# Writing f by pairs of images and moving the last f products ahead of the taps

## What is computed

```python
def first(x):                      # x = x + first(group_norm(x))
    f = relu(conv1x1(x, conv_w) + conv_b)                   # 256 -> 64 channels
    g = relu(mean_pixels(x) @ conv_w.T + conv_b)            # (16, 64)
    K = g[:, :, None] * wk + bk                             # a 5x5 kernel per image and channel
    W1 = relu(k0 * K + k1 * K.mean(0) + kb)                 # and W2, 3x3, in the same way
    y1 = depthwise(f, W1, 5x5) + adap_bias
    y2 = depthwise(f, W2, 3x3, dilation 2) + atrous_bias
    return conv1x1(concat(y1, y2), fuse_w) + fuse_b         # 128 -> 256 channels

def second(x):                     # x = x + second(group_norm(x))
    ...                            # halo attention, blocks of 8 x 8, windows of 16 x 16
    sim = where(mask, -max, q @ k + rel_pos)                # mask: positions inside the image
    out = softmax(sim) @ v @ Wout.T + Wout_b
```

## Time and profile before

| | |
|---|---|
| runs shown | 208.17, 208.6 and 210.85 us (median 208.6) |
| the profiled execution | 205.92 us, its span from first to last instruction 204.0 us |
| TensorE busy | 162.2 us, 80% of the span |
| VectorE, ScalarE, GpSimd busy | 151.0, 126.4, 89.0 us |
| bytes moved | 54.82 MB, mean 269 GB/s |
| chain that ended last | TensorE 64%, SyncE's queue 26%, copies of f 3% |

### The profile page before, as it was taken

How to read it: one execution, slowest core, us unless ns; L and a number is a source line. 1 busy time by engine, 2 the same in 40 slices (tenths; PEclk the granted TensorE clock), 3 DMA queues, 4 the chain that set the end, 5 groups by cost and what they waited for, 6 DMA issues and landing times.

```text
span 204.0 us, 3894 instructions
## 1 busy us (share of the span) xinstructions
PE 162.2 (80%) x1376; PEld 101.3 (50%) x1376; DVE 151.0 (74%) x342; ACT 126.4 (62%) x241; POOL 89.0 (44%) x139
## 2 busy tenths in 40 slices
PE   0001696966597999999999999999999999999430
PEld 0000322322256375676586676586586587584330
DVE  0198948888492418989989789899789899799930
ACT  2667469989346264775695585695495695444520
POOL 8802305050508304124337557328857417527530
PEclk9999999999999999999999999999999999999955
DMA  6999999999499999999637679996999998972997
GB/s 207 406 410 409 410 408 410 409 395 252 132 192 206 229 212 224 220 223 209 147 77 176 136 258 210 309 289 159 322 291 239 280 339 209 335 276 112 381 358 282
DMA packets 24466, 54.82 MB, mean 269 GB/s; under 512 B 2560, under 2 KB 14592, under 8 KB 22912
## 3 DMA queue, kind: packets, MB, share of 16 engines
q1 hardware_dynamic: 24032, 54.14, 87.5%
q10 hardware_dynamic: 416, 0.44, 0.9%
HBM read 32.78 MB, written 21.79 MB: 268 GB/s over the span
## 4 chain that ended last, share of the span: by engine, by line
PE 64%; SPq 26%; DMA 3%; issue 2%; ACT 1%; DVE 1%; POOL 1%; DVEq 0%; ACTq 0%
PE pt L819 29%; PE pf L831 28%; SPq L203 14%; SPq L215 9%; PE pf L757 3%; DMA fc<-fd 3%; PE px L856 3%; SPq L208 2%; PE px L845 1%; ACT junkt L455 1%; POOL cw L398 1%; SPq L224 0%; SPq L206 0%; DVE xs L182 0%; DVEq L66 0%
## 5 line engine op out<-in xcount | busy, mean ns | idle before, releaser
L458 ACT ACTIVATE junkt<-xs,sm 128x1024 bf16<-128x1024 f32 x31 | 35.6, 1149 | 37.7 <-DVE xs L672 37.7
L831 PE MATMUL pf<-reg,cst 128*128 128x512 f32 x128 | 58.8, 603 | 0.0
L672 DVE SCALAR_TENSOR_TENSOR xs<-pf,cst,xs 128x1024 f32<-128x1024 f32 x31 | 39.5, 1273 | 7.0 <-PE pf L831 7.0
L418 ACT ACTIVATE wa<-xs 128x1024 bf16<-128x1024 f32 x28 | 29.3, 1053 | 10.3 <-DMA xs<-x_dram 10.3
L654 DVE STREAM_TRANSPOSE reg<-pt 128x512 f32<-128x512 f32 x32 | 23.0, 717 | 17.1 <-PE pt L819 14.1
L831 PEld LDWEIGHTS pf<-reg,cst 128*128 128x128 f32 x128 | 23.0, 190 | 24.9 <-issue 24.4
L329 POOL TENSOR_TENSOR pre<-cst,sv 96x512 f32<-96x512 f32 x15 | 15.8, 1056 | 43.7 <-ACT wa L442 19.6
L819 PEld LDWEIGHTS pt<-fc,wa 96*64 96x64 f32 x512 | 27.8, 136 | 7.1 <-issue 5.3
L819 PE MATMUL pt<-fc,wa 96*64 96x128 f32 x512 | 29.8, 274 | 1.4 <-DMA fc<-fd 1.4
L819 PEld LDWEIGHTS pt<-fc,reg 96*64 96x64 f32 x512 | 27.9, 136 | 5.9 <-issue 5.9
L819 PE MATMUL pt<-fc,reg 96*64 96x128 f32 x512 | 29.7, 273 | 0.0
(11 more groups left out here) (102 smaller groups left out, 130.8 us busy)
## 6 DMA issues: line engine op xcount, KB each, us to landing
xs<-x_dram SPq DMA_DIRECT2D x16, 1024.0 KB, 18.6
fc<-fd SPq DMA_DIRECT2D x48, 306.0 KB, 5.3
out_dram<-xs SPq DMA_DIRECT2D x10, 1024.0 KB, 6.1
out_dram<-xs SPq DMA_DIRECT2D x12, 256.0 KB, 4.6
out_dram<-xs SPq DMA_DIRECT2D x6, 512.0 KB, 3.6
fd<-own SPq DMA_DIRECT2D x40, 76.5 KB, 5.6
fd<-reg SPq DMA_DIRECT2D x24, 76.5 KB, 4.6
cst<-columns_dram ACTq DMA_DIRECT2D x1, 304.0 KB, 4.3
```

The costliest lines, as they stand in the source:

```text
L418: act.activation(junkl[m % 2], plane(n, c), func, scale=scale, accum_out=dst).then_inc(s_xs, 1)
L458: act.activation(junk[m % 2], plane(n, c), ACT.Square, bias=nwb[:, c:c + 1], accum_out=accq[:, 1, m:m + 1]).then_inc(s_sq, 1)
L672: dve.scalar_tensor_tensor(out=plane(n, c), in0=pf[c][:, :], scalar=fb[:, c:c + 1], in1=plane(n, c), op0=ALU.add, op1=ALU.add, accum_out=r ...
L831: mm = pe.matmul(pf[c][:, h * HALF:(h + 1) * HALF], fw[:, 128 * c:128 * (c + 1)], y2[n % 2][:, h * HALF:(h + 1) * HALF], start=True, stop= ...
```

## The change

It does six things.

- The attention weights and `sx` get room of their own at the end of `reg`; their loads stay behind x in the queue.
- f is written to DRAM by pairs of images: one transfer of 128 partitions x 8 x 153 numbers in place of eight of 16 x 8 x 153. The channels of the convolution are permuted on the host so that the planes fall into place.
- A copy of f goes to partitions k, k + 4, k + 8, ... (k = 0, 1, 2) in place of 32 neighbours. The taps' operations run over 128 partitions in place of 96; every fourth partition has weights and data of zero. For that GpSimd sets both copy buffers to zero as a whole, ahead of its other memsets.
- TensorE's order changes: the attention product comes right after the first half of f pair 5, and pairs 6 and 7 come ahead of the taps of image 0.
- ScalarE's order follows: the attention matrix ahead of the taps' fourth channel, pairs 5 and 6 ahead of the weights of image 1.
- GpSimd's scaled weights of the last batch wait for the pixel means.

```diff
-KROWS = 96
+KROWS = 128
...
-        reg = sb("reg", [128, 3072 + WALL])
+        reg = sb("reg", [128, 3072 + WALL + 96])
...
-        wv, wot = fc[1][:, 0:512], fc[1][:, 512:1024]
-        sx = fc[1][0:64, 1024:1536].rearrange("p (n g v) -> p n g v", n=N, v=2)
+        wv, wot = reg[:, 3672:4184], reg[:, 4184:4696]
+        sx = reg[0:64, 4696:5208].rearrange("p (n g v) -> p n g v", n=N, v=2)
...
-            sp.wait_ge(s_fcz, 2)
             sp.dma_start(wv.rearrange("p (k c) -> p k c", k=2),
...
-            def write_f(n):
-                sp.wait_ge(s_fev, n // 2 + 1)
-                m = 64 * (n % 2)
-                for c4 in range(4):
-                    sp.dma_start(bass.AP(fd, n * IMG + c4 * SPLIT * SET, [[PLANE, GROUPS], [SET, SPLIT], [1, PLANE]]),
-                                 slots[n // 2][m + c4:m + c4 + 61:4, :].rearrange("p (h f) -> p h f", h=SPLIT)
-                                 ).then_inc(s_fw[n], 16)
+            def write_f(q):
+                sp.wait_ge(s_fev, q + 1)
+                sp.dma_start(bass.AP(fd, 2 * q * IMG, [[PLANE, 2 * CM], [2 * CM * PLANE, SPLIT], [1, PLANE]]),
+                             slots[q].rearrange("p (h f) -> p h f", h=SPLIT)).then_inc(s_fw[q], 16)
...
                 for k in range(3):
-                    sp.dma_start(fc[n % 2][32 * k:32 * k + 32, LEAD - k:LEAD - k + RUN],
-                                 bass.AP(fd, n * IMG, [[SET, 32], [1, RUN]])).then_inc(s_cp[n % 2], 16)
+                    sp.dma_start(fc[n % 2][k:k + 125:4, LEAD - k:LEAD - k + RUN],
+                                 bass.AP(fd, n // 2 * 2 * IMG + n % 2 * CM * PLANE,
+                                         [[2 * CM * PLANE, SPLIT], [SET, 4], [1, RUN]])).then_inc(s_cp[n % 2], 16)
...
             for b in range(2):
-                pool.memset(fc[b][:, RUN:COPY], 0.0).then_inc(s_fcz, 1)
+                pool.memset(fc[b][:, :], 0.0).then_inc(s_fcz, 1)
...
                 pool.wait_ge(s_rstd, k + 1)
+                if k == BATCHES - 1:
+                    pool.wait_ge(s_gm, BATCHES)
...
-            for q in range(2, 6):
+            for q in range(2, 5):
                 store_f(q)
+            act.wait_ge(s_atm, 1)
+            act.activation(at[:, :], pf[0][:, 0:HALF], ACT.Copy, scale=1.0 / KEYS).then_inc(s_at, 1)
...
+            store_f(5)
+            store_f(6)
             taps(1)
-            store_f(6)
             store_f(7)
```

More of the change, by code:

```diff
@@ L146, in build @@
         s_attw = sem("attention_weights_loaded")
-        s_fw = [sem(f"f_written{n}") for n in range(N)]
+        s_fw = [sem(f"f_written{q}") for q in range(N // 2)]
         s_cp = [sem(f"copies_landed{b}") for b in range(2)]
@@ L243, in inner_rows @@
                 store_rows(n, IN0, IN1)
-            for n in range(6):
-                write_f(n)
+            for q in range(2):
+                write_f(q)
+            sp.wait_ge(s_fcz, 2)
             copies(0)
[L248 to L251, removed]
             copies(1)
-            write_f(8)
-            write_f(9)
+            for q in range(2, 7):
+                write_f(q)
             for n in range(N):
@@ L658, in order_image @@
                 if n < 2:
-                    for q in range(2, 6):
-                        dve.wait_ge(s_fw[q], 64)
+                    for q in range(1, 3):
+                        dve.wait_ge(s_fw[q], 16)
                 else:
@@ L777, in _ @@
             f_pair(5, (0,))
[L778 to L787, removed]
-            pe.wait_ge(s_fev, 4)
-            pe.matmul(pf[0][0:KROWS, HALF + 64:HW], sel, flat[:, 64:512], start=True, stop=True).then_inc(s_smm, 1)
-            for c in range(NC2):
-                pe.matmul(pt0[:, 96 + c:97 + c], fw[:, 128 * c:128 * (c + 1)], yb, start=True, stop=True)
-            shifts(3)
-            pe.wait_ge(s_attw, 32)
+            pe.wait_ge(s_attw, 32)
+            pe.wait_ge(s_fev, 4)
             for c in range(NC2):
@@ L798, in _ @@
             mm.then_inc(s_atm, 1)
+            pe.wait_ge(s_gm, BATCHES)
+            for c in range(NC2):
+                mm = pe.matmul(px[:, 64:64 + N], cw[:, c, :], gm[:, c, :], start=(c == 0), stop=(c == NC2 - 1))
+            mm.then_inc(s_gmm, 1)
+            shifts(3)
+            for c in range(NC2):
+                pe.matmul(pt0[:, 96 + c:97 + c], fw[:, 128 * c:128 * (c + 1)], yb, start=True, stop=True)
+            pe.wait_ge(s_sx, 1)
+            flat = reg[0:64, 4696:5208]
+            pe.matmul(px[0:KROWS, 0:64], sel, flat[:, 0:64], start=True, stop=True).then_inc(s_smm, 1)
+            f_pair(5, (1,))
+            pe.wait_ge(s_sx, 2)
+            pe.matmul(pf[0][0:KROWS, HALF + 64:HW], sel, flat[:, 64:512], start=True, stop=True).then_inc(s_smm, 1)
+            f_pair(6)
+            f_pair(7)
             def taps(n, h):
@@ L906 @@
     mask16 = np.zeros((128, GROUPS), np.float32)
-    for ch in range(CM):
-        mask16[ch, ch // 4] = 1.0
-        for p in range(KROWS):
-            if p % 32 // 8 == ch % 4:
-                sel[ch, p] = 1.0
+    for q in range(CM):
+        mask16[q, q % GROUPS] = 1.0
+        for k in range(3):
+            sel[q, 4 * (q // GROUPS) + k:KROWS:16] = 1.0
+    perm = 4 * (np.arange(CM) % GROUPS) + np.arange(CM) // GROUPS
     group_mean = (row[:, None] // GROUP == row[None, :] // GROUP).astype(np.float32) / GROUP
```

27 lines of the change are left out of this document (10 added, 17 removed).

## The result

| | before | changed |
|---|---|---|
| median of the runs | 208.38 us (207.26 to 210.85, 4 runs) | 212.53 us (210.06 to 213.75, 4 runs) |
| ratio, 95% interval | | 1.0158 (1.0106 to 1.0211) |
| profiled execution, its span | 205.92 us, 204.0 us | 211.46 us, 209.5 us |
| start of the taps of image 1 | 73.34 us | 74.98 us |
| start of the taps of image 2 | 80.47 us | 84.34 us |

The changed kernel is 1.6% slower. The forecast was 209.5 us with a range up to 211.3, so the measured median lies above the range; one of the four runs, 210.06, lies inside it.

The account below looks back on a forecast made before the run. The end was taken to hang on when the taps of image 1 start, with TensorE at a fixed pace after. -3.1 (TensorE's order) + 4.0 (memset) = +0.9 us on 208.6 gave 209.5 us, range 204.4 to 211.3.

Parts of the forecast that it names:

- the memset holds VectorE: At the start, GpSimd's longer memsets hold VectorE's first constants from 9.48 to 13.4 us: +4.0 us.
- nothing takes the delay up: From VectorE's constants to TensorE's list: no wait absorbs the late start, so all 4.0 us arrive there.
- +0.9: Sum of the terms for the whole kernel: -3.1 us from TensorE's order and +4.0 from the memset.
- TensorE's order: Ahead of the taps, reordered products fill idle waits; taps of image 1 start at 70.25 against 73.34, 3.1 us earlier.
- f products at 0.215 us a record: TensorE ahead of the taps: each f product costed at 6.87 / 32 records, 1.72 us for a half pair.
- I take zero for all of this, and the cover is the 6.87 us of f products: Copies of images 0 and 1 land before needed, under cover of f pairs 6 and 7: no cost.
- a gap between tap groups: Named sign of a wrong forecast: gaps opening between TensorE's tap groups would mean copies come late.
- The rival that was priced by rate alone: Copies split over 8 of 16 transfer engines exceed 7.28 us an image: +25 us, 234 us; chance 0.06.
- 10.9 us with 5.3: Copies, in the half-engines rival: 10.9 us from issue to need, 5.3 to landing, some 5.6 us of lead.
- SyncE issues less: SyncE issues half a write of f per image in place of four, so its own time falls; counted as zero.

Follow-up runs that it names:

- run 3: Changed kernel with the two whole memsets of the copy buffers on VectorE ahead of its constants, not on GpSimd: 213.02 us, ratio 1.0301.
- run 10: Changed kernel with all edits of run 8, and f pairs 5, 6, 7 written behind the copies of images 2, 3, 4: 202.31 us, ratio 0.9776.
- run 7: Changed kernel with f pairs 6 and 7 back behind the taps of image 0 and the copy-buffer memsets on VectorE: 211.0 us, ratio 1.0136.
- run 2: Changed kernel with f written per image in two transfers per pair, so copies use all 16 engines: 207.9 us, ratio 1.0017.
- run 9: Changed kernel with only the writes of f pairs 5, 6, 7 moved behind the copies of images 2, 3, 4; copies on 8 engines: 215.33 us, ratio 1.0304.
- run 8: Changed kernel with copies on 16 engines, copy-buffer memsets on VectorE, and second half of f pair 5 right behind the means product: 208.79 us, ratio 1.0077.
- run 11: As run 10, but copies and writes of f keep the changed kernel's form, so copies run on 8 engines: 208.19 us, ratio 0.9911.

## Why the prediction was wrong

**Right: the memset holds VectorE.** 4.20 us were forecast as 4.0, and 13.4 us as its end. The sentence that nothing takes the delay up was too strong: 2.9 of it arrive ahead of the taps. That the taps of image 1 come 1.6 us late where +0.9 was forecast is in part luck: 1.1 us less from the memset stand against 1.8 more from the clock below. The Trainium skill ("SBUF — State Buffer", section "Who interferes with whom") says that a tensor_scalar can be held by a GpSimd instruction for its whole length; this trace agrees with 4.20 us beside the memset and 0.17 without it (run 3).

**Right: TensorE's order.** The engine followed the list, with the wait of 0.70 us ahead of the scales. In run 10, without memset and half clock, the taps of image 1 start 4.0 us earlier than before, which is the forecast's 3.1, the 0.70 of the gap that the filler closes, and 0.2 more.

**Left out: the granted clock.** The terms took f products at 0.215 us a record throughout. Behind products of 1 to 64 columns and a gap of 0.70 us the clock went to its lower level: +1.8. No row of before shows such a fall at that place, but its list had full products between the small ones, and the new list does not.

**The step that failed: "I take zero for all of this, and the cover is the 6.87 us of f products".** The step followed the copies of images 0 and 1 alone, and these were in time. The copies of image 2 wait for a buffer that the taps of image 0 free. Before, the f products of pairs 6 and 7 stood between those taps and the taps of image 2, which made 80.47 - 66.47 = 14.0 us, and the copies, issued from 69.29, still had 11.2 of it:

```profile
69.29 2.23 SPq L224 DMA_DIRECT2D fc<-fd  x3
```

Now the products stand ahead of both, and 82.05 - 74.95 = 7.1 are left, while the copies need 84.30 - 75.01 = 9.3 from first issue to landing. The products cannot cover the load of image 0 and that of image 2 at once. It cost 2.3 us of wait and 1.7 of half clock behind it, and those 4.0 us are what turns +1.6 into +5.6. It is the sign of being wrong that the prediction named: a gap between tap groups. The short window alone is not the cause: in run 10 one of 7 us was enough, and in run 7 one of some 14 was not. It takes the window and the late landing together.

**The rival that was priced by rate alone.** Copies on half of the engines had a chance of 0.06, with the condition that they decide where an image's transfers exceed 7.28 us. They do not: from 89.66 on no image waits, and in all the split cost 1.4% (run 2). The split itself came as that rival said; the Trainium skill ("DMA: Bandwidth & Descriptors", section "Why a DMA increments its semaphore by 16 and not by 1") has the rule, the largest number up to 16 that divides both outermost counts, and the trace agrees with 8 small packets a copy. What decided was the time from issue to landing of one set of copies, once, in a window of 7.1 us: 9.3 us, and 8.8 with nothing ahead of it in run 9. The prediction did compare a window with a landing time, 10.9 us with 5.3, but both were those of the kernel before; the change itself shortens the one and lengthens the other.

**SyncE's queue.** The prediction counted that SyncE issues less. It did not count what now stands ahead of the copies of image 2, two pair writes of 612 KB that used to stand behind. In the changed kernel that hides behind the slow copies; in run 8 it is worth 6.5 us.

**Open.** Each of the three edits of run 8 was not taken out of run 10 by itself, apart from the engines (run 11). The edit that gives the copies 16 engines also writes f per image in two transfers, and the two were not separated. Whether run 2 would wait for image 2 with the writes still on the way, as in the changed kernel, is not shown by its one profile. Why three issues of copies took 4.89 us in run 7 was seen beside full transfer engines, and not tested.

## What to carry to other kernels

Work that is moved out from between two uses of a double buffer takes away the time in which the buffer is refilled; measure the window from "free" to "needed" for the next refill, not only for the first. Compare it with the time from issue to landing, on as many transfer engines as the pattern's outermost counts allow, and with all that stands ahead in the queue. When one mended cost buys nothing, look for a second limit right behind the first before giving the first one up.

## What the runs showed of the hardware that was not expected

- A set of three copies, 918 KB, needed 8.8 us from its first issue on 8 engines with nothing ahead of it and a write behind it (run 9); on 16 engines, again with a write behind it, it was there within 5.5 (run 10). Single copies landed after 3.9 us in the median (run 2) where before they took 5.3.
- A wait of 2.3 us on TensorE was followed by taps at a granted clock of 0.69 that took 5.32 us in place of 3.65 (changed kernel): that wait cost 4.0 us in all, not 2.3. The waits of 1.15 and 2.12 us in run 11 were followed by taps of 3.73 and 3.72 us.
- A memset, which reads nothing, held a VectorE operation on two numbers a partition for 4.20 us.
